# Context transforms from paired rows, and an odd inverse transform and the expert ranks moved on TensorE

## What is computed

```python
seq = q.shape[1]                       # 512
Q = q @ Wq.T + bq                      # q: the normed, scaled rows of x
K = mem @ Wk.T + bk                    # mem: the context times a constant
V = mem @ Wv.T + bv
Qf = jnp.fft.fft(Q, axis=-2)
Kf = jnp.fft.fft(K, axis=-2)
Vf = jnp.fft.fft(V, axis=-2)
filt = jnp.exp(1j * ATT_ALPHA * jnp.arctan(jnp.log(kidx + EPS)))[None, :, None]
QK = hamilton(Qf * filt, Kf * filt)
QKV = hamilton(QK, Vf * filt)
attended = jnp.fft.ifft(QKV, axis=-2).real
x = x + attended                       # then the layer of experts on x
```

## Time and profile before

| | |
|---|---|
| median of 3 runs | 3343.62 us (3343.38 to 3343.95) |
| profiled execution | 3342.41 us |
| its span, first to last instruction | 3340.6 us |
| mean granted TensorE clock, as a share | 0.987 |
| TensorE busy | 3237.0 us, 97% |
| VectorE busy | 2799.1 us, 84% |
| ScalarE busy | 2238.1 us, 67% |
| GpSimd busy | 1300.1 us, 39% |

### The profile page before, as it was taken

The page is one execution under the profiler, slowest core; times in us unless marked ns, Lnnn a source line. Parts: engine busy times, 40 slices in busy tenths (PEclk is TensorE's granted clock), DMA queues, the critical chain, the costliest instruction groups (busy, mean ns, idle before and its releaser), DMA issues. The chain is left out here.

```text
span 3340.6 us, 54951 instructions
## 1 busy us (share of the span) xinstructions
PE 3237.0 (97%) x17944; PEld 2682.9 (80%) x17944; DVE 2799.1 (84%) x3891; ACT 2238.1 (67%) x4836; POOL 1300.1 (39%) x1608
## 2 busy tenths in 40 slices
PE   6999999999999999999999679999999999999998
PEld 5777777777777777777777369999999999999997
DVE  4999999999999999999999767777777777777774
ACT  5666666676766666666766367777777777777764
POOL 3456757666666667576665500000000000000001
PEclk9999999999999999999999789999999999999999
DMA  6432221222121222312130233333444343333431
GB/s 229 153 101 79 74 92 61 78 76 88 63 88 63 88 76 65 111 52 88 64 102 26 83 108 115 114 118 123 127 127 122 120 127 114 113 105 116 124 102 38
DMA packets 299918, 327.15 MB, mean 98 GB/s; under 512 B 47600, under 2 KB 179056, under 8 KB 299760
## 3 DMA queue, kind: packets, MB, share of 16 engines
q1 hardware_dynamic: 284400, 308.12, 29.0%
q0 software_dynamic: 15360, 16.99, 1.5%
HBM read 256.96 MB, written 101.97 MB: 107 GB/s over the span
## 5 line engine op out<-in xcount | busy, mean ns | idle before, releaser
L1424 POOL TENSOR_TENSOR tally<-tally,unit 1x1 f32<-1x1 f32 x16 | 8.4, 524 | 1286.0 <-DVE res L1871 1286.0
L1527 PE MATMUL out_ps<-wo_h,act_h 128*128 128x512 f32 x1024 | 403.3, 394 | 0.0
L1528 PE MATMUL out_ps<-wo_h,act_l 128*128 128x512 f32 x1024 | 403.0, 394 | 0.0
L1529 PE MATMUL out_ps<-wo_l,act_h 128*128 128x512 f32 x1024 | 398.5, 389 | 0.0
L1860 DVE TENSOR_TENSOR act_l<-act,act_h 128x512 fp32r<-128x512 f32 x256 | 176.5, 690 | 264.6 <-ACT act_h L1694 264.6
L1830 DVE TENSOR_TENSOR wi_l<-w_sum,wi_h 128x1024 fp32r<-128x1024 f32 x128 | 156.8, 1225 | 114.4 <-ACT wi_h L1626 113.3
L1468 PE MATMUL y_bank<-tok_h,wi_h 128*128 128x256 f32 x768 | 221.8, 289 | 5.4 <-DVE tok_l L1796 5.4
L1529 PEld LDWEIGHTS out_ps<-wo_l,act_h 128*128 128x128 f32 x1024 | 192.4, 188 | 43.0
L508 PE MATMUL pair<-w_qh,q_high 128*128 128x512 f32 x512 | 222.1, 434 | 1.5 <-ACT q_low L740 1.5
L1468 PE MATMUL y_bank<-tok_h,wi_l 128*128 128x256 f32 x768 | 217.7, 284 | 0.0
L1468 PE MATMUL y_bank<-tok_l,wi_h 128*128 128x256 f32 x768 | 217.5, 283 | 0.0
(11 more groups left out here) (244 smaller groups left out, 10924.9 us busy)
## 6 DMA issues: line engine op xcount, KB each, us to landing
w_raw<-in_L_ffn_wi SPq DMA_DIRECT2D x256, 256.0 KB, 2.9
w_raw<-in_L_ffn_wo SPq DMA_DIRECT2D x128, 512.0 KB, 4.8
w_raw<-in_x SPq DMA_DIRECT2D x32, 1024.0 KB, 5.3
w_raw<-in_ctx SPq DMA_DIRECT2D x32, 1024.0 KB, 5.3
x_res<-in_x SPq DMA_DIRECT2D x31, 1024.0 KB
out<-x_res SPq DMA_DIRECT2D x31, 1024.0 KB
slots<-rows SPq DMA_DIRECT2D x4, 4160.0 KB, 15.7
got<-slots SPq DMA_DIRECT2D x15, 1040.0 KB, 7.8
```

The lines of the kernel that those rows point to most:

```text
L1424: nc.gpsimd.tensor_tensor(tally[:], tally[:], unit[:], ALU.add).then_inc(tallied, 1)
L1527: nc.tensor.matmul(out_ps[t][:], ah, oh, start=(j == 0 and h == 0), stop=False)
L1528: nc.tensor.matmul(out_ps[t][:], al, oh, start=False, stop=False)
L1529: last = nc.tensor.matmul(out_ps[t][:], ah, ol, start=False, stop=(j == STEPS - 1 and h == 1))
```

## The change

**Odd frequencies of the context.** The sine and cosine of an odd frequency at row 256 - n are, up to the sign, those at row n. So with the differences d(n) of rows n and n + 256, the real part needs d(n) - d(256 - n) and the imaginary part d(n) + d(256 - n), for n from 0 to 127 with rows 0 and 128 treated apart. Each is 128 rows, and each matmul then makes 128 columns of one part instead of 256 of both: `fwd_o`'s cosines on one, the new `fwd_p`'s sines on the other. For this the context's rows 128, 255 to 129 and 384, 511 to 385 are needed in turned order; a second copy of them in that order, `ctx_back`, is laid out in DRAM before the launch.

**Loads and folds.** `context_rows` replaces the one load by four: rows 0 to 255 (semaphore `c_low_rows`), rows 256 to 383, and the two turned groups, the last into a new tile `c_back`. GpSimd then adds rows 256 to 511 onto rows 0 to 255 by a transfer with an addition (`add_rows`), after a multiply of one element, `c_tick`. VectorE's `folds_c` waits for all of it and has six instructions of 512 elements instead of two of 1024 and two of 512.

**Scratch tiles.** `unused` becomes one tile for each norm, and each sum waits for the sum ahead of it.

**Order on TensorE.** `ranks` moves from the end of a sequence's list to behind the first two removals of the next, and the odd inverse of the first half moves by one place.

```diff
@@ forward_paired, new
+def forward_paired():
+
+    m = forward_odd().reshape(128, 2, 256)
+    sine = m[:, 0, 128:].copy()
+    sine[0] = m[0, 1, 128:]
+    return sine
@@ xattn_moe_kernel
+    c_pair = nc.inline_tensor(np.outer(np.arange(P) > 0, [-1, 1]).astype(np.float32), "c_pair").ap()
-            unused = [[sb(f"unused{i}{j}", [P, DIM], bf16) for j in (0, 1)] for i in (0, 1)]
+            unused = [sb(f"unused{i}", [P, DIM], bf16) for i in (0, 1)]
@@ SP
+                    def context_rows(b):
+
+                        every = seq(ctx_in, b)
+                        sp.dma_start(c_in[:, 0:2], every[:, 0:2]).then_inc(c_low_rows, 16)
+                        sp.dma_start(c_in[:, 2], every[:, 2]).then_inc(c_loaded, 16)
+                        back = ctx_back[bass.ds(b, 1)].rearrange("a t p n -> p (a t) n")
+                        sp.dma_start(c_in[:, 3], back[:, 0]).then_inc(c_loaded, 16)
+                        sp.dma_start(c_back[:], back[:, 1]).then_inc(c_loaded, 16)
@@ SP, start
-                    sp.dma_start(c_in, seq(ctx_in, 0)).then_inc(c_loaded, 16)
+                    context_rows(0)
...
+                    sp.dma_start(fwd_p[:], c_fwd_p).then_inc(fwd_in, 16)
+                    sp.dma_start(paired[:], c_pair).then_inc(fwd_in, 16)
                     sp.dma_start(pos[:], c_pos).then_inc(pos_in, 16)
@@ TensorE, dft
                         for t in range(2):
+                            if w == 0:
+                                last = nc.tensor.matmul(ps[:, 256 + t * P:256 + (t + 1) * P], folded[:, 1, t, u * P:(u + 1) * P],
+                                                        fwd_p[:] if t else fwd_o[:, 0, 0:P], start=False, stop=True,
+                                                        skip_group_check=True)
+                                continue
@@ TensorE, body
                         remove_high(b - 1, 0, 1)
+                        ranks(b - 4)
                         dft(b - 1, 0, 2)
...
                         dft(b - 1, 1, 0)
+                        inverse(b - 3, 0, 1)
                         dft(b - 1, 1, 1)
                         remove_high(b - 1, 1, 0)
-                        inverse(b - 3, 0, 1)
                         remove_high(b - 1, 1, 1)
...
                         dft(b, 0, 1)
-                        ranks(b - 3)
@@ ScalarE, row_sum (square_sum likewise)
-                        if t > 1:
-                            act.wait_ge(sums, b * SUMS + t - 1)
-                        nc.scalar.activation(unused[t % 2][:], src[:, t, 0:DIM], ACT.Copy,
+                        if t > 0:
+                            act.wait_ge(sums, b * SUMS + t)
+                        nc.scalar.activation(unused[:], src[:, t, 0:DIM], ACT.Copy,
@@ GpSimd
+                    def add_rows(b):
+
+                        if not on(b):
+                            return
+                        pool.wait_ge(c_low_rows, b * 16 + 16)
+                        wait(pool, c_ticked, b)
+                        tv(c_tick[:], k["one"][0:1, 0:1], k["one"][0:1, 0:1], ALU.mult).then_inc(c_ticked, 1)
+                        nc.gpsimd.dma_start(c_in[:, 0:2], seq(ctx_in, b)[:, 2:4], accum_op=ALU.add).then_inc(c_summed, 16)
@@ GpSimd, body
                         scatter(b - 5, 1 - p)
+                        add_rows(b)
                         real_bins(b - 2)
@@ VectorE, folds_c
-                            fold(b, c_in, c_fold, cf_ready, (c_loaded, b * 16 + 16), b * 8 - 4)
-                            fold_again(b, c_in, c_fold, cf_ready)
+                            dve.wait_ge(c_loaded, b * C_LOADS + C_LOADS)
+                            dve.wait_ge(c_summed, b * 16 + 16)
+                            v.scalar_tensor_tensor(c_in[:, 2], c_in[:, 2], -2.0, c_in[:, 0], ALU.mult, ALU.add).then_inc(cf_ready, 1)
+                            v.tensor_tensor(c_in[:, 3], c_in[:, 3], c_back[:], ALU.subtract).then_inc(cf_ready, 1)
+                            wait(dve, f1_mm, b * 8 - 4)
+                            v.tensor_tensor(c_fold[:, 0, 0], c_in[:, 0], c_in[:, 1], ALU.add).then_inc(cf_ready, 1)
+                            v.tensor_tensor(c_fold[:, 0, 1], c_in[:, 0], c_in[:, 1], ALU.subtract).then_inc(cf_ready, 1)
+                            dve.wait_ge(cf_ready, b * FOLDS_C + 2)
+                            v.scalar_tensor_tensor(c_fold[:, 1, 0], c_in[:, 3], paired[:, 0:1], c_in[:, 2], ALU.mult, ALU.add).then_inc(cf_ready, 1)
+                            v.scalar_tensor_tensor(c_fold[:, 1, 1], c_in[:, 2], paired[:, 1:2], c_in[:, 3], ALU.mult, ALU.add).then_inc(cf_ready, 1)
```

More of the change, by code:

```diff
@@ L142, in wait, with xattn_moe_kernel @@
         engine.wait_ge(sem, value)
-def xattn_moe_kernel(nc, x, ctx_in, wq, wk, wv, bq, bk, bv, gate, gamma, beta, wi, wo, out):
+def xattn_moe_kernel(nc, x, ctx_in, ctx_back, wq, wk, wv, bq, bk, bv, gate, gamma, beta, wi, wo, out):
     f32, f32r, bf16 = mybir.dt.float32, mybir.dt.float32r, mybir.dt.bfloat16
@@ L186, in xattn_moe_kernel @@
             fwd_o = sb("fwd_o", [P, 2, 256])
+            fwd_p = sb("fwd_p", [P, 128])
+            paired = sb("paired", [P, 2])
             inv = sb("inv", [P, 2, 2, 256])
@@ L457, in dft @@
                         if isinstance(b, int) and b == 0 and w == 0 and u == 0:
-                            pe.wait_ge(fwd_in, 32)
+                            pe.wait_ge(fwd_in, 64)
                         unit = w * 4 + u
-                        folded, ready = ((c_fold, cf_ready), (q_fold, qf_ready))[w]
+                        folded, ready, folds = ((c_fold, cf_ready, FOLDS_C), (q_fold, qf_ready, FOLD))[w]
                         if u == 0:
-                            pe.wait_ge(ready, b * FOLD + FOLD)
+                            pe.wait_ge(ready, b * folds + folds)
                         if unit < 2 and on(b - 3):
@@ L644, in _ @@
                         body(b + 1, 1)
-                    for b in range(30, BATCH + 3):
+                    for b in range(30, BATCH + 4):
                         body(b, b % 2)
@@ L668, in square_sum @@
                             act.wait_ge(*mean)
-                        act.wait_ge(sums, b * SUMS + 4 + t - 1)
-                        nc.scalar.activation(unused[t % 2][:], src[:, t, 0:DIM], ACT.Square, bias=neg[:, t:t + 1],
+                        act.wait_ge(sums, b * SUMS + 4 + t)
+                        nc.scalar.activation(unused[:], src[:, t, 0:DIM], ACT.Square, bias=neg[:, t:t + 1],
                                              accum_out=into[:, t:t + 1]).then_inc(sums, 1)
@@ L1002, in _ @@
                     hc, uc, ro = Chain(dve, ham, HAM), Chain(dve, unfold, UNF), Chain(dve, route, ROUTE)
-                    def fold(b, src, dst, ready, source, users):
-                        dve.wait_ge(*source)
-                        wait(dve, f1_mm, users)
-                        v.tensor_tensor(dst[:, 1], src[:, 0:2], src[:, 2:4], ALU.subtract).then_inc(ready, 1)
-                        v.tensor_tensor(src[:, 0:2], src[:, 0:2], src[:, 2:4], ALU.add).then_inc(ready, 1)
                     def fold_again(b, src, dst, ready):
@@ L1031, in folds_c @@
                         if on(b):
-                            fold(b, c_in, c_fold, cf_ready, (c_loaded, b * 16 + 16), b * 8 - 4)
-                            fold_again(b, c_in, c_fold, cf_ready)
+                            if isinstance(b, int) and b == 0:
+                                dve.wait_ge(fwd_in, 64)
+                            dve.wait_ge(c_loaded, b * C_LOADS + C_LOADS)
[8 more added lines that the diff above has]
+                            v.scalar_tensor_tensor(c_fold[:, 1, 1], c_in[:, 2], paired[:, 1:2], c_in[:, 3], ALU.mult, ALU.add).then_inc(cf_ready, 1)
                     def low_weights():
```

20 lines of the change are left out of this document (13 added, 7 removed).

## The result

The changed kernel takes 3334.7 us in the median of 11 runs (3333.5 to 3337.1), the kernel before 3343.3 beside it (11 runs). The ratio is 0.9974, with a 95% interval of 0.9965 to 0.9983. So it is faster, but by 8.6 us and not by the 19 of the forecast.

A forecast was written before the change was run, and what follows sets the result against it. TensorE was taken to set the 57.54 us period per sequence; minus 1.8, plus 0.95, plus 0.1 for waits gives 56.8. Over 31 periods 23 us less, minus 4 at the start, gives 3324 us, range 3303 to 3341.

The forecast's parts named there:

- TensorE's path: TensorE's work per sequence in the attention part sets the period: 57.54 - 1.8 + 0.95 = 56.7 us, 56.8 with waits.
- the transfer: Adding transfer on GpSimd: issue costs nothing, lands at 943 to 950.6, taken as 946, so VectorE's folds don't wait.
- Context transforms: TensorE's context units: eight passes of 128 columns, 0.88 us, saving 0.42 us a unit, 1.7 a sequence.
- Ranks behind the two removals: TensorE's context part: third unit starts at about T + 2.5, query part at 6.5; with narrower units 1.8 us saved.
- The odd inverse: TensorE's query part: inverse ahead of a unit lengthens the stretch to 5.76 us, 0.95 more; VectorE's 1.4 us wait goes.
- VectorE's path: VectorE's work per sequence, new folds included: 56.3 us (55.5 to 56.35), below TensorE's.
- ScalarE's sums: One scratch tile makes each sum wait for the last: 0.13 us a gap, 1.6 us of ScalarE a sequence.
- the ring: Cycle from VectorE's add through GpSimd's mean and statistics, ScalarE's squares and `real_row`, back to VectorE; serial sums add 0.8 to 1.2 us.
- The second rival: Four-engine cycle through the serial sums and `real_row` sets the period at 57.1 to 57.6 us: 3335 to 3347; chance 0.13.
- The signs: Right: period 56.7 to 57.0, nearly 1 us TensorE wait in two pieces; wrong: VectorE waiting over 0.5 us for `real_row`.
- Start: GpSimd's first mean, later behind `pos`, tick and adding transfer, delays the first projection: +4 us, once.
- The first rival: VectorE is the bound at 56.2 us or less a sequence: 38 us less, 3306; chance 0.17.

The follow-up runs named there:

- run 1: Changed kernel with the odd inverse put back between the removals of query units 0 and 1: 3323.1 us, ratio 0.9938, period 56.65 us.
- Run 4: Kernel before with only the odd inverse moved ahead of the second query transform: 3372.8 us, ratio 1.0087, period 58.55 us.
- run 10: Changed kernel, odd inverse left at its new place, with two scratch tiles for each pair of sums (four in all): 3332.0 us, ratio 0.9965.
- run 6: Changed kernel with the odd inverse back at its old place and four one-byte scratch tiles for the sums: 3307.9 us, ratio 0.989, period 56.07 us.
- run 8: Changed kernel without the adding transfer and its tick, upper context rows left out of the sums: 3329.8 us, period 57.04 us.
- run 7: Changed kernel with the odd inverse back and ScalarE's last square of the result put behind pair 2's work and two token blocks: 3420.7 us, ratio 1.0218.
- run 3: Changed kernel with both TensorE moves, odd inverse and ranks, undone: 3356.5 us, ratio 1.0039.

## Why the prediction was half right

- **Direction and mechanism: right.** TensorE's path is the period (runs 1, 4, 10), the folds cost nothing, the wait for the inverse goes, the transfer doesn't delay the folds. The gain is 8.6 us where 19 were forecast. The step that failed is a term of TensorE's sum, the 1.8 us for the narrower context units with the ranks' move: it measures 1.55. A second term, 3.3 us at the end of the attention part, was not in the sum at all.
- **Context transforms: right.** Four passes at 0.11 stand where four at 0.215 stood (932.22, 932.44). The first unit, among the projections, gives 0.41 (978.82 to 979.71 for 981.99 to 983.29), 0.42 was said.
- **Ranks behind the two removals: overestimated.** The third unit starts 2.58 behind the second, where the prediction had 2.5, and the query part at T + 6.73, where it had 6.46. Together 0.39 + 0.75 + 0.41 = 1.55 us come off. Of the 0.27 too much at the query part, 0.15 is a slip in the prediction's own working: it says that it sets 0.05 against the saving of units three and four, and then takes 0.1 off instead, for which it gives no reason. With the 0.05 put on it would have said 6.61. Another 0.08 is the third unit: the first removal behind the second unit is followed by a wait of 0.39 for `c_high`, and with the ranks' 0.50 behind the second one the low copy is no longer waited for. The last 0.04 lies among units three and four.
- **The odd inverse: nearly exact.** The inverse takes 1.72 (939.81 to 941.53; 1.73 was said), the stretch 5.68 against 5.76. The stretch behind it is 0.11 longer, which the sum didn't have. The next odd inverse shows its end, before and then after:

```profile
952.25 1.88 PE L542 MATMUL odd_ps<-r_spec,inv 128*128 128x512 f32 x4
```

```profile
949.08 1.88 PE L573 MATMUL odd_ps<-r_spec,inv 128*128 128x512 f32 x4
```

  From the third query unit to it are 952.25 - 947.46 = 4.79 us before and 949.08 - 944.18 = 4.90 after. So the cost is 5.68 - 4.80 + 0.11 = 0.99 in place of 0.95. Run 4 measures 58.55 - 57.56 = 0.99 by itself.
- **TensorE's path.** 57.54 - 1.55 + 0.99 = 56.98, and 57.05 was measured, where the prediction had 56.7, and 56.8 with its allowance of 0.1 for waits (0.07 is left for it here). 0.25 came from the ranks' step and 0.04 from the inverse's. The period is 0.25 longer than forecast, 31 x 0.25 = 8 us.
- **VectorE's path: right.** 57.05 - 0.78 = 56.27, forecast 56.3; without any wait it is 56.07 (run 6). The section that the prediction quotes here (the Trainium skill, VectorE: DVE Perf Modes, The DRAIN you can't avoid) goes on that an instruction which is not held starts earlier, so it is not stricter than the rows. The new folds start 0.60 to 0.73 us apart and last 0.68 to 0.80, so each starts before the one ahead of it has ended.
- **ScalarE's sums: right here, but not for the next bound.** The step grew by 0.14 (949.77 to 950.52 is 0.75, against 0.61), 0.13 was said. They cost the changed kernel 2.7 us in all (run 10), since TensorE is slower than the ring. The second rival named the ring and put it at 57.1 to 57.6. Run 1 finds it at 56.65, below TensorE's path as the change left it and above it as soon as the inverse goes back.
- **The signs.** One sign of being wrong came true, VectorE waiting over 0.5 us for `real_row` (0.78), though the second rival, which it was to show, does not hold: by run 10 that wait comes from TensorE. Of the new waits of TensorE the prediction had the one at the second query removal (0.46), but no wait shows at the third query unit, and the 0.39 at the second context removal was not foreseen. The period of 57.04 lies just above the 56.7 to 57.0 named.
- **Start: right.** 4.1 us, forecast 4.
- **The end: missing from the sum.** From the last `real_in` (1863.35 before, 1852.52 after) to the end the changed kernel takes 3.3 us more. 2.2 is GpSimd's queue at the hand-over (run 8). The last sequence's own sums and squares stand bare there: GpSimd waits 11.83 us for them where it waited 11.43, and 3.53 where it waited 3.10, 0.8 in all. But run 8 has the same serial sums and takes only 0.15 more than the kernel before in this part (1477.40 against 1477.25), so how the last 1.1 us divide stays open.
- **The sum again, with these terms:** 31 x (57.54 - 57.05) = 15.2, minus 4.1, minus 3.3, is 7.8; the profiled spans differ by 7.5.
- **The first rival (VectorE as the bound)** is what the change would have been without the inverse's move and with four tiles: 56.07 and 3307.9, where it said 3306.

## What to carry to other kernels

When two engines are almost full, moving a piece to an earlier place in one engine's list is a cost to be weighed against the wait that it filled before: the inverse's move bought VectorE nothing that the narrower passes and the ranks' move hadn't already given it (in run 1 VectorE doesn't wait for the odd inverse), and cost TensorE 1 us a sequence. Work out the second-longest ring with the new order and not the old one, and test each part of a composite change in the presence of the others, since here the same memory saving cost 3, 15 or 33 us, and the same move of the ranks 0, 10, 16 or 33. If room for scratch output is short, a narrower type for what is never read gives it back without a wait.

## What was not expected of the hardware

- **A GpSimd step on four elements a partition lasts 0.20 us alone and up to 2.36 beside VectorE's products of 128x2048.** In run 1 the step at 951.20 ends at 953.40, the product that began 0.15 before it at 953.34; the next one likewise. By the rule of the Trainium skill, SBUF — State Buffer, section SBUF: two separate sides, whichever of a VectorE instruction with two inputs in SBUF and a GpSimd instruction that reads SBUF starts first holds the port for its whole length; these rows agree. What surprised is the leverage: 0.85 us of work put behind in ScalarE's list became 4 us a sequence in run 7 (60.5 against 56.65), where a chain of short steps moved from a gap into the products.
- **An adding transfer of 512 KB lands 6.1 us after its issue**, a plain one of the same size from SP in 3.8. The 3.2 us that the prediction worked out by the Trainium skill, DMA: Bandwidth & Descriptors, section Anatomy of one DMA, is half of it; whether the addition makes the difference no run shows, since none has a plain transfer of this size from GpSimd. Taking the transfer out shortens GpSimd's idle time where its part of the program ends from 4.29 to 2.05 us (run 8).
- **TensorE's granted clock fell behind waits of 0.9 to 2 us in some sequences and not in others.** It is 1.00 through the steady part of the changed kernel with its two waits of 0.4 and 0.5. In run 3 it is 0.72 behind a wait of 0.87, though 1.00 behind the one of 0.94 (998 to 1005 us). In run 7 it is 0.65 behind 2.13 with 0.63 more close after. At the lower level, 1.2 GHz, a pass of 128 columns takes 0.21 instead of 0.11.
- **The first even passes of a unit can take about 0.1 us longer at the full clock.** In the rows of the changed kernel it is 0.53 at 934.35, straight behind the ranks, and 0.55 at 944.18, behind the removal that had waited, against 0.44 at 938.50. It makes most of the 0.11 above. What causes it is not shown.
